# A gated cross-attention block followed by two local-attention layers: the opening stage re-ordered, its norms moved between engines, and the split of the first layer's weights spread over it

## What is computed

```python
# cross-attention
Q = layernorm(x) @ Wq + bq;  K = ctx @ Wk + bk;  V = ctx @ Wv + bv
probs = softmax(where(mask == 0, -inf, Q K^T / sqrt(256)))
context = probs @ V
x = x + tanh(g_xattn) * (norm(context) * ln_gamma + ln_beta)
# two layers on y = layernorm(x), rows of two batches form windows of 128
h = shift_token(y);  q, k, v = split(h @ wqkv);  q, k = rotary(l2norm(q) * qs, l2norm(k) * ks)
y = y + local_attention(q, k, v) @ wo
h = norm(shift_token(y)) * ln_g + ln_b
a, g = split(h @ w1 + b1);  y = y + (a * gelu(g)) @ w2 + b2
# then
x = x + tanh(g_ffn) * y
```

## Time and profile before

| what | value |
|---|---|
| median of 3 runs | 792.92 us (789.53 to 794.18) |
| the profiled execution | 791.66 us |
| span in its profile | 789.9 us |
| busy PE, DVE, ACT, POOL | 722.1, 531.9, 481.3, 436.0 us |
| granted TensorE clock, mean | 0.964 of full speed |
| first result `x1` of step 0 | 161.76 us after the span's start |

### The profile page before, as it was taken

How to read it: one execution, slowest core, us unless ns; L and a number is a source line. 1 busy time by engine, 2 the same in 40 slices (tenths; PEclk the granted TensorE clock), 3 DMA queues, 4 the chain that set the end, 5 groups by cost and what they waited for, 6 DMA issues and landing times.

```text
span 789.9 us, 17103 instructions
## 1 busy us (share of the span) xinstructions
PE 722.1 (91%) x4952; PEld 599.1 (76%) x4952; DVE 531.9 (67%) x1486; ACT 481.3 (61%) x1291; POOL 436.0 (55%) x592
## 2 busy tenths in 40 slices
PE   6988964999999999999999899999999999999967
PEld 5777753787878787878787777878787878787847
DVE  2798897286757575858575955757575757575732
ACT  2343622468585858585857684757575757585742
POOL 1433454465575656656565565748484747474722
PEclk9999985799999999999999999999999999999988
DMA  7444330451101010101010001010101010101000
GB/s 210 153 146 155 102 68 29 146 199 44 41 2 40 0 40 0 40 0 40 9 31 13 27 1 54 2 54 0 53 0 53 0 53 0 53 0 41 1 28 13
DMA packets 32786, 38.36 MB, mean 49 GB/s; under 512 B 8476, under 2 KB 22896, under 8 KB 32752
## 3 DMA queue, kind: packets, MB, share of 16 engines
q1 hardware_dynamic: 32752, 37.95, 15.1%
HBM read 29.55 MB, written 8.39 MB: 48 GB/s over the span
## 4 chain that ended last, share of the span: by engine, by line
PE 57%; issue 7%; DVE 7%; ACT 5%; POOL 4%; DMA 1%; ACTq 0%; SPq 0%; DVEq 0%; POOLq 0%
PE ps L423 34%; PE ps L625 4%; PE ps L584 3%; PE ps L611 3%; POOL pr L1389 3%; PE ps L602 2%; PE ps L596 2%; PE ps L629 2%; ACT pr L870 2%; PE ps L518 2%; PE ps L613 1%; PE ps L612 1%; PE ps L416 1%; DVE hT_lo L1140 1%; ACT hT_hi L909 1%
## 5 line engine op out<-in xcount | busy, mean ns | idle before, releaser
L1389 POOL TENSOR_SCALAR pr<-pr,rl 128x128 f32<-128x128 f32 (+1 forms) x256 | 107.7, 434 | 78.2 <-DVE rl L1173 77.5
L870 ACT ACTIVATE pr<-sm,mn 128x128 f32<-128x128 f32 (+1 forms) x256 | 113.6, 448 | 15.4 <-DVE mn L1167 14.6
L423 PE MATMUL ps<-hT_hi,w_hi 128*128 128x256 f32 (+1 forms) x352 | 105.4, 299 | 3.6 <-DVE hT_lo L1140 1.4
L1167 DVE CUSTOM_DVE_ANT_0 sm<-ps,wmask 128x128 f32<-128x128 f32 (+1 forms) x256 | 80.1, 355 | 35.0 <-PE ps L602 30.3
L423 PE MATMUL ps<-hT_hi,w_lo 128*128 128x256 f32 (+1 forms) x352 | 100.3, 285 | 0.0
L423 PE MATMUL ps<-hT_lo,w_hi 128*128 128x256 f32 (+1 forms) x352 | 99.4, 282 | 0.0
L1355 POOL TENSOR_TENSOR rn<-ss,nhalf 128x16 f32<-128x16 f32 x32 | 95.9, 2998 | 2.7
L830 ACT ACTIVATE sqb<-ps 128x512 f32<-128x512 f32 x64 | 37.9, 595 | 89.9 <-PE ps L423 83.6
L423 PE MATMUL ps<-wqkv_hi,yT_hi 128*128 128x512 f32 x192 | 80.1, 417 | 7.7 <-DVE arena L1012 5.1
L423 PE MATMUL ps<-wqkv_lo,yT_hi 128*128 128x512 f32 x192 | 77.2, 402 | 0.0
L423 PE MATMUL ps<-wqkv_hi,yT_lo 128*128 128x512 f32 x192 | 77.2, 402 | 0.0
(11 more groups left out here) (156 smaller groups left out, 2132.7 us busy)
## 6 DMA issues: line engine op xcount, KB each, us to landing
arena<-x SPq DMA_DIRECT2D x16, 256.0 KB, 3.6
ystream<-arena SPq DMA_DIRECT2D x16, 256.0 KB, 2.0
y_next<-ystream SPq DMA_DIRECT2D x16, 256.0 KB, 2.7
y_res<-ystream SPq DMA_DIRECT2D x16, 256.0 KB, 2.6
arena<-L_ffn_w SPq DMA_DIRECT2D x6, 640.0 KB
arena<-ctx SPq DMA_DIRECT2D x8, 256.0 KB, 3.9
arena<-mask_BxSxS_ik SPq DMA_DIRECT2D x8, 256.0 KB, 2.7
xmid<-arena SPq DMA_DIRECT2D x8, 256.0 KB, 2.0
```

What stands on the lines that cost most here:

```text
L423: last = mm(out, lhsT(a), rhs(b), start=(start and i == 0), stop=(stop and i == 2))
L870: A(pr[:, h % NS, a:b], sm[:, h % NS, a:b], ACT.Exp, bias=mn[:, h, t:t + 1], scale=-1.0, accum_out=ls[:, h, t:t + 1]).then_inc(e_done, 1)
L1167: V.tensor_tensor_reduce(sm[:, h % NS, a:b], bank(h % SB)[:, a:b], wmask[:, a:b], 1.0, -NEG, ALU.add, ALU.min, mn[:, h, t:t + 1]).then_inc ...
L1389: G.tensor_scalar(pr[:, h % NS, a:b], pr[:, h % NS, a:b], rl[:, h, t:t + 1], 1.0, ALU.mult, ALU.mult).then_inc(pn_done, 1)
```

## The change

- **Turns**: all ten are written out, on every engine.
- **Input norm**: DVE keeps the statistics (`input_statistics`, now placed before `add_context`). POOL makes the scale and the shift (`input_rstd`, four small operations), and ACT normalises (`normalise_input`, two operations at the end of its turn).
- **Context norm**: its statistics are taken from the unnormalised product in PSUM. `context` subtracts the mean and multiplies by gamma in one fused operation for each half, and `add_context` scales and adds the residual in another. The softmax sum enters through `square_sums` on POOL, two small operations that add eps times the squared sum to the variance. The reciprocal, `gate_context` and one pass over the tile leave DVE.
- **Weights of layer 0**: ACT makes one `hi` piece of `wqkv`/`wo` in each of turns 2 to 5, and `w2` in turn 6; POOL makes one `lo` piece at the end of each of turns 3 to 6, and `w2` in turn 7. `w2` is loaded into `pT` in turn 2.
- **Constants**: four loads at the end of each of SP's turns 3 to 6. **Rotary tables**: one layer's in turn 3 and one's in turn 4, on POOL.
- **w1 of layer 0** is loaded after turn 8; its offset products stand in the middle of step 0 (before the head transposes), in PSUM bank 5, its scaling on POOL before the last batch's `context_rstd`. **w1 of layer 1**: offset products and scaling move from the first step of layer 1 to step 1.
- **w1 split** (both layers): within the loop over heads of the layer's first step (ACT after heads 3 and 5, DVE after heads 4 and 6), no longer behind it.

```diff
@@ run_x @@
-            turn(0, True, False, False, True)
...
-            with eng.Fori(3, NB - 1) as b:
-                turn(b, True, True, True, True)
...
+            for b in range(NB + 2):
+                turn(b, b < NB, 1 <= b <= NB, b >= 2, b < NB - 1)
+                if b <= NB:
+                    between(b + 1)
@@ SP, end of a turn @@
+                if b == 2:
+                    load_layer(0, 3)
+                if b == NB:
+                    for semaphore, count in ((xn_tr, NB), (q_mm, NB), (k_mm, NB), (v_mm, NB), (mb_done, NB)):
+                        sp.wait_ge(semaphore, count)
+                    load_layer(0, 2)
+                if 3 <= b < 7:
+                    n = 4 * (b - 3)
+                    load_constants(small[12:][n:n + 4])
@@ PE, step @@
                 if A:
                     project(1, (2,))
+                if first:
+                    bias_products(0)
...
-                        if isinstance(s, int) and s in (0, NB) and h == HEADS - 1:
-                            bias_products(la)
+                        if isinstance(s, int) and s == 1 and h == HEADS - 1:
+                            bias_products(1)
@@ ACT, turn @@
+                if 2 <= b < 2 + FIRST:
+                    high_part(0, "wa", b - 2)
+                elif b == 6:
+                    high_part(0, "wc", 0)
+                    high_part(0, "wc", 1)
                 if project:
                     projected(1)
+                if ahead:
+                    normalise_input(b + 1)
+            def normalise_input(n):
+                act.wait_ge(x_shift, n + 1)
+                wait(act, xn_tr, n)
+                for t in range(T):
+                    A(xn[:, t, :], x_in[:, t, :], ACT.Identity, bias=xmr[:, t:t + 1],
+                      scale=xrs[:, 0, t:t + 1]).then_inc(xn_done, 1)
@@ ACT, loop over heads @@
+                        if isinstance(s, int) and s in (0, NB) and h in (3, 5):
+                            high_part(la, "wb", (h - 3) // 2)
@@ DVE @@
             def context(b):
                 dve.wait_ge(ctx_mm, b + 1)
-                dve.wait_ge(rlx, b + 1)
-                wait(dve, tg_done, b)
+                statistics(1, b, halves(7))
+                dve.wait_ge(var[1], T * (b + 1))
                 for t in range(T):
-                    V.tensor_scalar(xc[:, t, :], halves(7)[:, t, :], xrl[:, t:t + 1], None,
-                                    ALU.mult).then_inc(xc_done, 1)
+                    V.scalar_tensor_tensor(xc[:, t, :], halves(7)[:, t, :], xmv[:, 1, t, 0:1], gam_bc[:],
+                                           ALU.subtract, ALU.mult).then_inc(xc_done, 1)
+            def add_context(b):
...
+                dve.wait_ge(rstd_done[1], b + 1)
+                dve.wait_ge(xrb_done, b + 1)
+                wait(dve, xmid_stored, 16 * b)
+                for t in range(T):
+                    last = V.scalar_tensor_tensor(x_mid[:, t, :], xc[:, t, :], xrs[:, 1, t:t + 1],
+                                                  x_res[:, t, :], ALU.mult, ALU.add)
+                last.then_inc(xmid_done, 1)
@@ POOL, turn @@
                 if finish:
                     context_rstd(b - 2)
+                if ahead:
+                    input_rstd(b + 1)
+                if b == 3:
+                    turning_tables(0)
+                if b == 4:
+                    turning_tables(1)
+                if weigh:
+                    square_sums(b - 1)
+                if finish:
                     rstd_x(2, b - 2)
-                if ahead:
-                    rstd_x(0, b + 1)
+                if 3 <= b < 3 + FIRST:
+                    low_part(0, "wa", b - 3)
+                elif b == 7:
+                    low_part(0, "wc", 0)
+                    low_part(0, "wc", 1)
```

More of the change, by code:

```diff
@@ L378, in step @@
                 f = s - 1
-                if isinstance(s, int) and s == 0:
-                    load_layer(0, 2)
                 if isinstance(s, int) and s == 1:
-                    sp.wait_ge(w_ready, VPIECES)
-                    sp.wait_ge(w2_ready, 2)
-                    for part in range(3):
+                    sp.wait_ge(wb_low, KC)
+                    for part in (2, 0, 1, 3):
                         load_layer(1, part)
@@ L752, in _, with high_part @@
             A = nc.scalar.activation
-            def high_parts(l, first, which=slice(None)):
-                act.wait_ge(wa_in if first else wb_in, 16 * (2 if first else WB_PARTS) * (l + 1))
-                if l:
-                    act.wait_ge(wo_mm if first else dn_mm, NB)
-                for i, (full, high, low) in list(enumerate(pieces(l, first)))[which]:
-                    if not first and i >= LAST_W2 - FIRST:
-                        act.wait_ge(w1_scaled, KC * l + i + 1 - (LAST_W2 - FIRST))
-                    A(high, full, ACT.Copy).then_inc(w_high, 1)
-                    if not first and i == 1:
-                        A(w2_hl[0][GT:GT + HT, HC - 1, :], full, ACT.Copy).then_inc(w2_copied, 1)
+            def high_part(l, part, i):
+                loaded, made = {"wa": (wa_in, wa_high), "wb": (wb_in, wb_high), "wc": (wc_in, wc_high)}[part]
+                act.wait_ge(loaded, 16 * {"wa": 2, "wb": WB_PARTS, "wc": 2}[part] * (l + 1))
+                if l and part == "wa":
+                    act.wait_ge(wo_mm, NB)
+                if l and part == "wc":
+                    act.wait_ge(dn_mm, NB)
+                if part == "wb":
+                    act.wait_ge(w1_scaled, KC * l + i + 1)
+                    if l:
+                        act.wait_ge(up_mm, HC * NB)
+                full, high, low = pieces(l, part)[i]
+                A(high, full, ACT.Copy).then_inc(made, 1)
+                if part == "wc" and i == 1:
+                    A(w2_hl[0][GT:GT + HT, HC - 1, :], full, ACT.Copy).then_inc(w2_copied, 1)
             def turn(b, project, weigh, finish, ahead):
@@ L883, in step @@
                 if isinstance(s, int) and s == NB:
-                    high_parts(1, True)
+                    for i in range(FIRST):
+                        high_part(1, "wa", i)
                 def normalise_rows():
@@ L1027, in turn, with low_part @@
                     V.tensor_scalar(mbias, m_in, 0, NEG, ALU.is_equal, ALU.mult).then_inc(mb_done, 1)
+                if ahead:
+                    input_statistics(b + 1)
                 if finish:
                     add_context(b - 2)
[L1030 to L1049 removed]
+                    mid_statistics(b - 2)
+                    normalise_mid(b - 2)
+            def low_part(l, part, i):
+                made, ready, n = {"wa": (wa_high, wa_low, FIRST), "wb": (wb_high, wb_low, KC)}[part]
+                full, high, low = pieces(l, part)[i]
+                dve.wait_ge(made, n * l + i + 1)
+                V.tensor_tensor(low, full, high.bitcast(F32), ALU.subtract).then_inc(ready, 1)
             def fold_offset(l):
                 dve.wait_ge(b1_mm, l + 1)
[L1054 removed]
+                sums = ps[:, b1_bank[l], 0:2 * HC].rearrange("p (h c) -> p h c", h=2)
                 V.tensor_tensor(b1_sb[:, l, :, 0:HC - 1], b1_sb[:, l, :, 0:HC - 1], sums[:, :, 0:HC - 1],
@@ L1210, in step @@
                 if isinstance(s, int) and s == NB:
-                    low_parts(1, True)
+                    for i in range(FIRST):
+                        low_part(1, "wa", i)
                 if F:
@@ L1376, in scale_w1 @@
                     wait_apart(pool, pool_passed, (b1_mm, l + 1))
+                    w1_in = raws(l)[2]
                     for k in range(KC):
[L1378 removed]
+                        G.tensor_scalar(w1_in[:, k, :], w1_in[:, k, :], lgb[:, l, 0, k:k + 1], 1.0,
                                         ALU.mult, ALU.mult).then_inc(w1_scaled, 1)
[L1381 to L1384 removed]
                 def normalise(h):
```

217 lines of the change are left out of this document (100 added, 117 removed).

## The result

| what | before | after |
|---|---|---|
| median | 792.4 us (4 runs, 789.5 to 794.2) | 804.3 us (4 runs, 800.1 to 805.2) |
| ratio, 95% interval | | 1.0151 [1.012, 1.0183] |
| the profiled execution, span | 791.66, 789.9 us | 803.86, 801.7 us |
| store of `y_new` of batch 5 | 96.79 us | 118.16 us (forecast 117.4) |
| first scores' minimum of step 0 (DVE) | 133.42 us | 150.70 us |

What follows compares the result with a forecast made beforehand. The prediction took the chain from the store of `y_new` through the residual's load to the next `y_new` as the bound. Step 0 +9.7, step 1 −1.7, step 8 +2.2, step 9 −4.0 gave +6.2: 799 us, range 785 to 805.

Steps and rivals of the forecast that it cites:

- the ring: In the turns: store of `y_new`, residual load, POOL's add, DVE's next `y_new`; claimed to bind, 11.3 us now, 10.6 after.

## What to carry to other kernels

Before moving small work into idle time, find the ring that ties a store to the next load, and ask of each queue which instructions are its members: a load whose issue takes 0.5 us is paid in full every turn behind the wrong store, and one wait later it costs nothing in the turn. Where two engines' operations hold each other up, put the long piece behind the short one with an explicit wait. And where a block becomes ready late, such as a scaling that waits for a DMA, put it last on its engine's queue: here that one exchange of lines was worth 1%. And a wait that an insert adds on PE has a second price, the clock behind it: the same 2.4 us wait was followed by 6.8 to 9.7 us of the same work, so one trace is not enough to price such an insert.
